# Moving the projection's eviction and the mask on ScalarE's queue in a graph attention and expert kernel

## The reference

```python
x = x + gnn(layernorm(x), adj, W, a)          # x: (64, 128, 128), adj: (64, 128, 128) of 0 and 1
x = x + ffn(layernorm(x), gate_w, gate_b, W1, b1, W2, b2)

def gnn(h, adj, W, a):
    Wh = h @ W
    s1, s2 = Wh @ a[:128], Wh @ a[128:]
    e = leaky_relu(s1[:, :, None] + s2[:, None, :], 0.2)
    return softmax(where(adj > 0, e, -9e15), axis=2) @ Wh

def ffn(x, ...):
    probs = softmax(x @ gate_w + gate_b)      # 8 experts
    # the two largest, with their probabilities as weights (not normalised again)
    # sum over the two of weight * (gelu(x @ W1[e] + b1[e]) @ W2[e] + b2[e])
```

## Time and profile before

| what | value |
|---|---|
| median of 3 timed runs | 420.98 us (417.93 to 421.82) |
| the profiled execution, its time | 417.27 us |
| its span in the trace | 415.4 us |
| mean granted TensorE clock | 0.853 of full speed |
| busy: PE, DVE, ACT, POOL | 326.1, 242.2, 245.1, 186.3 us |
| first stage (to the last sort landed) | 0 to 199 us |
| second stage | 199 us to the end |

### The profile page before, as it was taken

One profiled execution on the slowest core, in us unless ns is written; L12 is line 12 of the kernel. 1 busy time (PEld: TensorE's weight loads), 2 busy tenths in 40 slices (PEclk: granted clock), 3 DMA queues, 4 the chain that ended last, 5 costly groups with the idle time before them and its releaser, 6 DMA issues.

```text
span 415.4 us, 9313 instructions
## 1 busy us (share of the span) xinstructions
PE 326.1 (79%) x2362; PEld 291.6 (70%) x2362; DVE 242.2 (58%) x1003; ACT 245.1 (59%) x779; POOL 186.3 (45%) x204
## 2 busy tenths in 40 slices
PE   7397776979768754220499999999999999999990
PEld 4185655757657444110399999999999999899990
DVE  4226858696694688661045656556655666566650
ACT  3254574563754431000378888778877887888860
POOL 5601400246756548877034444444444444444441
PEclk9759779697796586555599999999999999999996
DMA  7943003067911001111111222222221211212100
GB/s 210 305 102 90 13 0 103 1 178 153 137 41 41 26 30 45 46 53 59 46 32 47 59 56 60 60 60 67 61 66 55 66 50 49 54 53 60 45 3 0
DMA packets 42231, 27.85 MB, mean 67 GB/s; under 512 B 5224, under 2 KB 40070, under 8 KB 42182
## 3 DMA queue, kind: packets, MB, share of 16 engines
q1 hardware_dynamic: 37222, 18.69, 18.4%
q0 software_dynamic: 4960, 8.58, 6.9%
HBM read 16.78 MB, written 12.23 MB: 70 GB/s over the span
## 4 chain that ended last, share of the span: by engine, by line
PE 57%; POOL 16%; issue 10%; ACT 6%; DVE 5%; DMA 3%; SPq 1%; POOLq 0%; ACTq 0%; DVEq 0%
PE at_ps L1150 21%; PE wh_ps L1129 17%; POOL sorted_rows L319 12%; PE wh_ps L1019 3%; PE at_ps L1148 3%; PE at_ps L1066 3%; POOL rstd L328 2%; ACT wh L381 2%; PE q_ps L1119 2%; PE q_ps L1058 1%; PE q_ps L1046 1%; ACT hid L501 1%; PE q_ps L1043 1%; DMA xt<-sorted_rows 1%; DVE rows L588 1%
## 5 line engine op out<-in xcount | busy, mean ns | idle before, releaser
L346 POOL DMA_INDIRECT out_x<-o_sb,xt x91 | 89.4, 982 | 120.6 <-DVE o_sb L952 119.6
L501 ACT ACTIVATE hid<-wh_ps,pair_w 128x128 f32<-128x128 f32 x364 | 103.7, 369 | 18.0 <-PE wh_ps L1129 17.8
L1150 PE MATMUL at_ps<-experts,hid 128*128 x728 | 111.1, 287 | 0.0
L1129 PE MATMUL wh_ps<-xnT,pair_w 128*128 128x128 f32 x728 | 98.6, 279 | 0.0
L1150 PEld LDWEIGHTS at_ps<-experts,hid 128*128 128x128 f32 x728 | 95.9, 192 | 2.5
L1129 PEld LDWEIGHTS wh_ps<-xnT,pair_w 128*128 128x128 f32 x728 | 90.1, 195 | 0.3
L319 POOL DMA_INDIRECT sorted_rows<-rows,pos x64 | 62.1, 971 | 42.5 <-DVE pos L756 25.1
L962 DVE COPY pair_w<-experts 128x258 f32 x182 | 54.1, 297 | 31.9 <-issue 19.9
L949 DVE SCALAR_TENSOR_TENSOR o_sb<-at_ps,xt 128x128 f32<-128x128 f32 x91 | 31.9, 351 | 66.5 <-PE at_ps L1150 65.8
L510 ACT ACTIVATE xn<-xt 128x128 f32<-128x128 f32 x91 | 44.4, 488 | 26.6 <-DMA xt<-sorted_rows 24.9
L1148 PE MATMUL at_ps<-experts,ones_bf 65*128 x182 | 40.9, 225 | 3.1 <-ACT hid L501 3.0
(11 more groups left out here) (170 smaller groups left out, 426.2 us busy)
## 6 DMA issues: line engine op xcount, KB each, us to landing
xt<-sorted_rows SPq DMA_DIRECT2D x91, 66.5 KB, 1.8
xin<-in_x SPq DMA_DIRECT2D x8, 512.0 KB, 4.6
adj_sb<-in_adj SPq DMA_DIRECT2D x8, 512.0 KB, 5.5
sorted_rows<-no_row SPq DMA_DIRECT2D x1, 1862.0 KB, 17.2
out_x<-o_sb,xt POOLq DMA_INDIRECT x91
experts<-in_L_ffn_W SPq DMA_DIRECT2D x1, 1024.0 KB, 6.8
experts<-in_L_ffn_W SPq DMA_DIRECT2D x2, 512.0 KB, 8.2
sorted_rows<-rows,pos POOLq DMA_INDIRECT x64, 2.3
```

Of the source, the lines that this page charges most:

```text
L346: nc.gpsimd.indirect_dma_start(out=out_v, out_offset=bass.IndirectOffsetOnAxis(ap=xt[:, n % XR, TOK:TOK + 1].bitcast(I32), axis=0), in_=o_ ...
L501: last = nc.scalar.activation(hid[:, n % WR, q, :], wh_ps[:, n % WR, q * P:(q + 1) * P], ACT.Gelu, bias=pair_w[:, n % WR, k, B1 + c:B1 + c ...
L1129: last = nc.tensor.matmul(wh_ps[:, n % WR, q * P:(q + 1) * P], pair_w[:, n % WR, k, c * P:(c + 1) * P], xnT[:, n % 2, :], start=True, stop ...
L1150: last = nc.tensor.matmul(at_ps[:, n % 2, cols], hid[:, n % WR, k * HC + c, :], experts[:, bass.ds(e, 1), W2C + c * P:W2C + (c + 1) * P], ...
```

## The change

In ScalarE's queue three things move. `copy_wh` of group i+3 no longer stands at the end of period i; it is done a period later, as `copy_wh(i+2)` of the next i, right behind the two `copy_probsT(i)`. `make_mask(i+2)` goes from right behind `copy_probsT(i)` to the end of the period, behind `copy_xT(i+3)`. In period 0 `make_mask(2)` goes behind `copy_xT(3)`, and `copy_wh(3)` goes to period 1. So `copy_s(i+1)`, the first of the next period, has `make_mask` ahead of it and no longer `copy_wh`. No instruction is added or removed, and the code of the other engines is the same.

```diff
                     copy_scores(1, 1)
-                    make_mask(2)
                     copy_xT(2, 0)
                     copy_xT(2, 1)
-                    copy_wh(2)
-                if 1 <= i and i + 2 < NG:
-                    make_mask(i + 2)
+                if i + 2 < NG:
+                    copy_wh(i + 2)
                 if i >= 2:
                     copy_rank(i - 2)
                 if i >= 1:
@@ -475,7 +473,8 @@
                 if i + 3 < NG:
                     copy_xT(i + 3, 0)
                     copy_xT(i + 3, 1)
-                    copy_wh(i + 3)
+                if i + 2 < NG:
+                    make_mask(i + 2)
```

## The result

The changed kernel takes 406.8 us in the median of 4 runs (405.03 to 411.75), the kernel before 420.94 beside it: a ratio of 0.966, 95% interval 0.959 to 0.973. Run again beside three experiments it took 407.65 us for 418.12, a ratio of 0.974 (0.970 to 0.978). So the two comparisons give 3.4% and 2.6%, 14.1 and 10.5 us. The kernel before has medians of 418.1 to 418.6 us in the 11 to 19 runs that stand beside the experiments, so the 420.94 of four runs is on the high side, and 10.5 us is the better figure for the gain. The profiled execution took 405.03 us with a span of 403.0, against 417.27 and 415.4 before.

A forecast was written before the change was run, and what follows sets the result against it. GpSimd's last 43.5 us of the first stage follow group 4's places, set by the attention periods, where TensorE waits for s_rows. Gains 2.5 + 1.9 + 1.2 + 3.5 + 2.7 = 11.8 us, from 420.98 to 409.2 us; range 403.5 to 414.5.

The forecast's parts named there:

- What bounds the stage: End of the first stage: GpSimd's unbroken 43.5 us of sorts and rstd, starting once group 4's places are known, shifts as a whole.
- Startup, 2.5 us: Period 0: projection 0.4 us earlier without the mask before xT; first score matmul at about 53.25 us instead of 55.79.
- Scores to the attention of period 1, 1.9 us: First score matmul to DVE's first row of period 1: 5.5 us instead of 7.38, with more at full clock.
- The two steps together, 4.4: Up to gate_sum of period 1: startup's 2.5 us plus 1.9 us from the scores to the attention.
- The cap by DVE and GpSimd: Periods 1 to 4: the loop gate_sum, norms, rstd, gate_sum limits periods to 14.92, then 15.30 us; gains 1.2 and 3.5.
- Period 4 to 5, 2.7 us: gate_sum to gate_sum: 14.3 us expected, between the loop's 13.40 and 14.94 for TensorE's chain at the old clock.
- Period 5 to 6, nothing: No gain, since no wh stood ahead of s_rows and TensorE waits for DVE's split_s; at most 2.35 us.
- The eviction's new place costs nothing; without its cover 2.1 us would be lost again: ScalarE's wh copy lies beside TensorE's attention at no cost; uncovered, its 2.6 us delays turn_x, losing about 2.1 us.
- The rival of a clock that eats part: TensorE idles ahead of project, clock falls through the scores, periods about 16.3 us: gain 5.4 us, 415.6 us; chance 0.18.
- The three cases that it counts as faster: Whole kernel: the forecast (gain 9 to 14 us, 0.55), clock stays up (14 to 16, 0.17), clock eats part (4 to 9, 0.18).
- the rival of a slower kernel: TensorE idle in two places each period stays at 1.2 GHz throughout: about 15 us slower, 436 us; chance 0.03.
- nothing is due: GpSimd's sorts beside a busier DVE: no delay expected, as sorts follow at 1.25 or 1.26 us either way; port rival 0.01.

## Why the prediction was right

It said 409.2 us (403.5 to 414.5), 11.8 us faster, and 406.8 was measured, then 407.65. The profiled pair differs by 12.2 us, the medians by 14.1 and 10.5. The 420.98 from which it subtracts is some 2.5 us above the later medians of the kernel before. By its steps:

- **What bounds the stage.** Right. GpSimd's 43.5 us shifted as a whole, to 141.73 for the 142.4 forecast.
- **Startup, 2.5 us.** Right: 2.6. The projection begins 1.89 us behind the start of the transposes (41.88 and 43.77) for 2.37 before, and the first score matmul 0.63 us behind the transpose of the score columns (51.68 and 52.31) for 2.74. That matmul is 3.48 us earlier in all. The other 0.9 is luck: in the projection at 43.77, which took 2.77 us for 3.62, the clock came back earlier, and in the eight traces that share the change's order in period 0 it took between 2.77 and 4.23.
- **Scores to the attention of period 1, 1.9 us.** Mis-sized. From 52.31 to DVE's first row at 58.78 it is 6.47 us and not 5.5: the clock fell at 55.1 us, between the scores and the transposes, and came back at 58.5. The gain of this step was 0.9. The 0.9 of luck ahead of it and 0.3 behind it (from DVE's first row to `gate_sum`, 1.09 us for 1.40) covered the shortfall.
- **The two steps together, 4.4.** The profile of the kernel before was of an early start. Two later kernels with the same code up to there have `gate_sum` of period 1 at 67.55 and 67.70 and not 64.57, with a projection of 3.90 and 3.78 us in place of 2.22 at 51 us. With the change's order in period 0, six traces have it at 59.8 to 60.6 and two at 63.0 and 63.3. Early for early and late for late, the difference is 4.0 to 4.8 us, but one early and one late execution would have shown 1.3 or 7.8.
- **The cap by DVE and GpSimd.** Right to 0.03 us in periods 1 to 2 and 2 to 3 (14.89 and 15.32 for 14.92 and 15.30), and shown by the two runs with the longer loop, 1.61 us a period after and nothing before. This was the crux, since TensorE's wait alone would have promised 2.1 us. Period 3 to 4 took 15.52 and not 15.30 for a reason that it put at nothing, told in the last section.
- **Period 4 to 5, 2.7 us.** Near one bound or the other: 3.43 in one profile, down at the loop's 13.40 plus 0.2, and 2.01 in the other (15.03, at the other bound of 14.94). In the first the clock stayed up from 102.9 to 123.4 us, in the second it was down from 113.3 to 120.1. Where TensorE's chain is the bound, the execution decides.
- **Period 5 to 6, nothing.** Right, and it is where the next piece lies: TensorE idles 5.43 us for DVE's `split_s` and then works at 1.2 GHz.
- **The eviction's new place costs nothing; without its cover 2.1 us would be lost again.** Right in both, the second by the run that took the cover away (17.05 for 15.3, the whole 1.7 that had been won).
- **What the prediction missed.** It treated the wait for `s_rows` as the price and the clock as a risk. The run with nine unused matmuls in the old wait shows that the clock by itself would have given the same periods. The sum was right since either path ends at the same cap.
- **The rival of a clock that eats part.** It did not happen, though TensorE does idle ahead of the projection (1.90 us at 62.70), as it said: the stretch at 1.2 GHz fell on the scores, the transposes and the attention, not on the projection, and even where it was 6.8 us long the chain needed 14.92 of the loop's 15.3 us.
- **Two sums that do not come out.** The three cases that it counts as faster have 0.90 together, so 0.92 is too high for them. In the rival of a slower kernel, 12 us of work at 1.9 times is 22.8 and not 20, which makes that rival about 447 us and not 436. The forecast does not rest on either.

## What to carry to other kernels

When a period shrinks because one wait goes, work out the other loops that the old period hid, each from one instruction back to itself in the next period; the longest of them is the new period, and here it capped the gain at 1.7 us of 2.1. On an engine with a strict queue, moving an instruction ahead of a long one only helps if the long one then lies beside work that nobody waits for: the same eviction gave periods of 17.0 us behind the router's exponential, 16.3 to 17.0 behind `xT` with `s_rows` ahead of it, and 14.9 to 15.5 behind the transposed probabilities. Before a wait is called the price, look at TensorE's clock behind it; filling the wait with unused matmuls is a cheap experiment that separates the two. And before a step is compared between two profiles, look whether they started alike: here the start of one and the same code differs by 3 us.

## What the runs showed of the hardware

**A sort and DVE got in each other's way.** DVE and GpSimd in period 3 of the changed kernel, and two DVE rows and a sort of the kernel before:

```profile
92.66 1.28 DVE L560 SCALAR_TENSOR_TENSOR lrelu<-scores 128x512 f32<-128x512 f32 x2
...
95.05 0.36 DVE L550 CAST s_cols<-wh 128x16 fp32r<-128x16 f32 x1
```
```profile
92.86 1.31 POOL L319 DMA_INDIRECT sorted_rows<-rows,pos  x1 [0.30 <-issue]
94.47 0.96 POOL L319 DMA_INDIRECT sorted_rows<-rows,pos  x1 [0.31 <-issue]
```
```profile
100.28 1.28 DVE L561 SCALAR_TENSOR_TENSOR lrelu<-scores 128x512 f32<-128x512 f32 x2
...
102.67 0.17 DVE L551 CAST s_cols<-wh 128x16 fp32r<-128x16 f32 x1
```
```profile
100.01 0.95 POOL L319 DMA_INDIRECT sorted_rows<-rows,pos  x1 [0.30 <-issue]
```

The sort that starts just inside the leaky relu, which reads the scores twice, takes 1.31 us for 0.96, and the small cast that starts inside the next sort takes 0.36 for 0.17. It is so again a period later (a sort of 1.31 us at 108.38, a cast of 0.36 at 110.58). The cast's 0.19 us is the difference between the periods of 15.52 and 15.32, and the prediction's "nothing is due" was off by that in periods 3 to 4 and 4 to 5. Before, a sort also lay on the leaky relu, but it had begun first, at 100.01 for 100.28, and then neither was longer (0.95 and 1.28 us); no sort lay on the cast. The Trainium skill's page "SBUF — State Buffer", section "Who interferes with whom", has it that a DVE instruction with two SBUF inputs contends with a GpSimd instruction that reads SBUF, and that the order of issue decides which of the two is held. The trace agrees where the sort came second. Where the leaky relu came second it shows no delay, and that the cast is held by the same port is not shown.

**The clock fell while TensorE was busy.** TensorE in two stretches of the changed kernel (length, busy, instructions, granted clock, DMA share, GB/s):

```profile
66.00:69.00 3.00, 2.74 (x14) 0.96 0.34 84
69.00:72.00 3.00, 3.00 (x14) 0.50 0.01 3
```

It had been idle for 0.26 us in the 3 us ahead of the fall, and it did the scores in them, most of whose matmuls use 32 rows of the array. Ahead of them it had idled for 1.90 us, before the projection; but in the run that filled that gap with seven matmuls the clock fell as well, at 69.9 us. In the run with nine full matmuls ahead of the scores it stayed up through the same work in period 3 and fell later in periods 2 and 4. What lets it fall is not shown beyond that.

**The start of the second stage varies by some microseconds.** The changed kernel in two executions, 195 to 200 us:

```profile
195.00:200.00 5.00, 4.29 (x37) 0.99 0.13 31
```
```profile
195.00:200.00 5.00, 4.46 (x22) 0.50 0.23 58
```

In the first the clock is up 4.8 us after the stage's first transpose (190.27 to 195.1), in the second 10 us after it (192.14 to 202.0). Behind the last sort the two have 218.7 and 220.3 us, so this can be 1.6 of the 3.5 us between their spans; the other 1.9 lie in the first stage, nearly all in periods 4 to 6, where the clock was down for longer.
